# Reading three partial sums back one by one at the end of a decoder layer: wider additions, and a gate product moved ahead of the last slot's turn

## The reference, cut to what matters

```
logits  = h @ gate_w.T; top 4 of 16 experts, weights normalised
shared  = (silu(h @ sg_gate.T) * (h @ sg_up.T)) @ shared_down.T      # 704 wide
shared *= sigmoid(h @ shared_gate_vec.T)
sparse  = sum over experts e: cw[:, e] * (silu(h @ g_e.T) * (h @ u_e.T)) @ down_e.T   # 176 wide
x       = x + shared + sparse
```

## Time and profile before

| what | value |
|---|---|
| median of 3 runs | 1036.52 us (1035.57 to 1037.06) |
| the profiled execution's own time | 1036.78 us |
| its span, first to last instruction | 1035.0 us |
| mean granted TensorE clock | 0.974 of full speed |
| TensorE busy | 964.0 us (93%) |
| VectorE busy | 827.1 us (80%) |
| GpSimd busy | 508.4 us (49%) |
| ScalarE busy | 379.7 us (37%) |

### The profile page before, as it was taken

One profiled execution on the slowest core, in us unless ns is written; L12 is line 12 of the kernel. 1 busy time (PEld: TensorE's weight loads), 2 busy tenths in 40 slices (PEclk: granted clock), 3 DMA queues, 4 the chain that ended last, 5 costly groups with the idle time before them and its releaser, 6 DMA issues.

```text
span 1035.0 us, 17365 instructions
## 1 busy us (share of the span) xinstructions
PE 964.0 (93%) x5569; PEld 852.9 (82%) x5569; DVE 827.1 (80%) x1595; ACT 379.7 (37%) x1063; POOL 508.4 (49%) x384
## 2 busy tenths in 40 slices
PE   4799899999999999999899999978999899999996
PEld 3688788889888887888788888866887799999985
DVE  4989999999889999878899988766576666666637
ACT  2454443533423443233353322341243244444420
POOL 0525344465635245666435667505715166666650
PEclk8899999999999999999999999989999999999999
DMA  9789679997248312203412120323141277777759
GB/s 348 279 326 380 248 270 366 408 344 274 87 148 307 131 62 82 78 27 115 192 61 83 62 83 22 149 95 130 63 184 69 67 122 117 119 121 120 121 78 304
DMA packets 67383, 171.84 MB, mean 166 GB/s; under 512 B 6752, under 2 KB 40288, under 8 KB 66144
## 3 DMA queue, kind: packets, MB, share of 16 engines
q1 hardware_dynamic: 52848, 151.69, 40.1%
q0 software_dynamic: 14448, 19.05, 11.2%
HBM read 84.72 MB, written 85.99 MB: 165 GB/s over the span
## 4 chain that ended last, share of the span: by engine, by line
PE 64%; DVE 25%; issue 5%; DMA 3%; ACT 1%; another core or an unknown queue 1%; SPq 0%; DVEq 0%; POOLq 0%; ACTq 0%
PE bank L469 8%; PE bank L471 8%; PE bank L470 8%; DVE rot L1335 5%; PE bank L549 5%; PE bank L679 4%; DVE rot L1332 4%; PE bank L702 4%; PE bank L818 3%; PE bank L820 3%; PE bank L779 3%; PE bank L572 2%; PE bank L574 2%; PE bank L573 2%; DMA raw<-in_wqkv 2%
## 5 line engine op out<-in xcount | busy, mean ns | idle before, releaser
L1145 POOL TENSOR_TENSOR rot<-turn 64x512 f32<-64x512 f32 x64 | 92.2, 1440 | 258.1 <-DVE turn L1319 232.9
L1319 DVE SCALAR_TENSOR_TENSOR turn<-bank,bqk,trig 128x1024 f32<-128x1024 f32 x128 | 160.7, 1276 | 13.2 <-PE bank L471 11.2
L1213 POOL DMA_INDIRECT sums<-ysb,token_at x79 | 123.1, 1558 | 76.1 <-DVE ysb L1686 37.1
L469 PE MATMUL bank<-xt_hi,w_hi 128*128 128x512 f32 x256 | 106.6, 417 | 16.7 <-DVE turn L1319 11.4
L1178 POOL TENSOR_TENSOR kv<-c_t,v_t 128x512 f32<-128x512 f32 x64 | 69.3, 1099 | 98.3 <-ACT v_t L945 46.0
L679 PE MATMUL bank<-wo,z_t 128*128 128x256 f32 x512 | 116.0, 379 | 0.8 <-ACT z_t L1016 0.8
L679 PEld LDWEIGHTS bank<-wo,z_t 128*128 128x128 f32 x512 | 94.9, 190 | 12.8 <-ACT z_t L1016 1.0
L977 ACT ACTIVATE prob<-prob,negmax 128x128 f32<-128x128 f32 x256 | 98.9, 389 | 6.9 <-DVE negmax L1304 6.8
L471 PE MATMUL bank<-xt_hi,w_lo 128*128 128x512 f32 x256 | 100.7, 393 | 0.0
L470 PE MATMUL bank<-xt_lo,w_hi 128*128 128x512 f32 x256 | 100.5, 392 | 0.0
L987 ACT COPY v<-bank 128x512 f32<-128x512 f32 x64 | 37.6, 587 | 164.6 <-PE bank L471 164.6
(11 more groups left out here) (183 smaller groups left out, 2424.0 us busy)
## 6 DMA issues: line engine op xcount, KB each, us to landing
xs<-zeros SPq DMA_DIRECT2D x12, 3710.0 KB, 17.1
w_hi<-w_dram SPq DMA_DIRECT2D x24, 768.0 KB, 4.7
w_lo<-w_dram SPq DMA_DIRECT2D x24, 768.0 KB, 7.0
xe_all<-xs SPq DMA_DIRECT2D x79, 132.5 KB
sums<-zeros SPq DMA_DIRECT2D x3, 2176.0 KB, 12.5
raw<-in_wqkv SPq DMA_DIRECT2D x16, 384.0 KB, 4.4
w_dram<-w_hi SPq DMA_DIRECT2D x8, 768.0 KB, 5.9
w_dram<-w_lo SPq DMA_DIRECT2D x8, 768.0 KB, 7.3
```

Source lines behind the costliest of these rows:

```text
L469: nc.tensor.matmul(o, lh, rh, start=(i == 0), stop=False)
L1213: nc.gpsimd.indirect_dma_start(sums_dram[s % YBUFS], bass.IndirectOffsetOnAxis(ap=token_at[:, s:s + 1], axis=0), ysb[s % YBUFS][:], None, ...
L1319: last = nc.vector.scalar_tensor_tensor(turn_all[m][:, 2 * i:2 * i + 2, :], qk_bank[2 * m + i][:].unsqueeze(1).to_broadcast([128, 2, GT]), ...
```

## The change

- The reads of the sums follow the landing of each array. The arrays' last slots are 76 (array 1), 77 (array 2) and 78 (array 0). SyncE now waits for array 1, issues four loads of it (four batches, 512 KB each), then the same for array 2 and for array 0. There are 12 loads in place of 24.
- VectorE adds four batches at a time, 12 additions of 128x1024 in place of 24 of 128x512: array 1 behind chunks 1 and 2, array 2 behind chunks 3 and 4 (two additions each), array 0 (four additions) behind chunk 5. A store of x now waits for the third array's addition to its quarter.
- `ysb` has four buffers (YBUFS) while the arrays stay three (SUMS); `slot_out(s)` waits for the landing of slot s - 4.
- The first gate product of the last quarter moves from s = 80 to s = 79, behind `slot_down(77)` and ahead of `slot_turn(78)`; its up product follows `slot_turn(78)`. For that the last quarter's chunks use the other bank of each pair (`shared_bank`), and two waits are set one slot earlier.

```diff
-YBUFS = 3
+YBUFS = 4
+SUMS = 3
+LAST_SUMS = [(SLOTS + i) % SUMS for i in range(SUMS)]
...
+def shared_bank(k, i):
+    return (i + (SLOTS if k == GROUPS - 1 else 0)) % 2
...
-            for i in range(YBUFS):
-                sp.wait_ge(y_stored[i], 16 * ((SLOTS - i + YBUFS - 1) // YBUFS))
-
-            for j in range(BATCH // 2):
-                for i in range(YBUFS):
-                    rows = sums_dram[i][j * 256:(j + 1) * 256, :]
-                    sp.dma_start(ys[j][:, i], rows.rearrange("(b p) d -> p b d", b=2)).then_inc(ys_loaded[j], 16)
-            for j in range(BATCH // 2):
-                sp.wait_ge(comb_done, YBUFS * (j + 1))
-                if 2 * j >= BATCH - GB:
-                    sp.wait_ge(acc_added, 2 * j + 2)
-                sp.dma_start(out[:, 2 * j:2 * j + 2, :], x[:, 2 * j:2 * j + 2, :]).then_inc(stored, 16)
+            for i in LAST_SUMS:
+                sp.wait_ge(y_stored[i], 16 * len(range(i, SLOTS, SUMS)))
+                for j in range(GROUPS):
+                    rows = sums_dram[i][j * GT:(j + 1) * GT, :]
+                    sp.dma_start(ys[j][:, i], rows.rearrange("(b p) d -> p b d", b=GB)).then_inc(ys_loaded[i][j], 16)
+            for j in range(GROUPS):
+                sp.wait_ge(comb_done, GROUPS * (SUMS - 1) + j + 1)
+                for half in range(2):
+                    b = GB * j + 2 * half
+                    if j == GROUPS - 1:
+                        sp.wait_ge(acc_added, b + 2)
+                    sp.dma_start(out[:, b:b + 2, :], x[:, b:b + 2, :]).then_inc(stored, 16)
...
-            def shared_up(k, i):
+            def shared_up(k, i, gates=True, ups=True):
                 n, q = k * SCH + i, SHARED_AT[k]
+                at = shared_bank(k, i)
+                if not gates:
+                    pe.wait_ge(eht_taken, SLOTS - 1)
+                    shared_block(SCH - 1 + i, banks[4 + at], q).then_inc(upb_ready, 1)
+                    return
...
-                if s == SLOTS + 1:
-                    unit(GROUPS - 1, 0)
                 if s >= 2:
                     slot_down(s - 2, experts[(s - 2) % 4])
+                if s == SLOTS:
+                    shared_up(GROUPS - 1, 0, ups=False)
                 if 1 <= s <= SLOTS:
                     slot_turn(s - 1)
+                if s == SLOTS:
+                    shared_up(GROUPS - 1, 0, gates=False)
...
-                if s >= YBUFS:
-                    pool.wait_ge(y_stored[s % YBUFS], 16 * (s // YBUFS))
+                if s >= SUMS:
+                    pool.wait_ge(y_stored[s % SUMS], 16 * (s // SUMS))
...
-                    dve.wait_ge(y_stored[s % YBUFS], 16 * (s // YBUFS))
+                    dve.wait_ge(y_stored[(s - YBUFS) % SUMS], 16 * ((s - YBUFS) // SUMS + 1))
...
-            def combine(j):
-                xj = x[:, 2 * j:2 * j + 2, :]
-                dve.wait_ge(ys_loaded[j], 16 * YBUFS)
-                for i in range(YBUFS):
-                    if i:
-                        dve.wait_ge(comb_done, YBUFS * j + i)
-                    nc.vector.tensor_tensor(xj, xj, ys[j][:, i], ALU.add).then_inc(comb_done, 1)
+            def combine(nth, j):
+                xj = x[:, GB * j:GB * (j + 1), :]
+                dve.wait_ge(ys_loaded[LAST_SUMS[nth]][j], 16)
+                if nth:
+                    dve.wait_ge(comb_done, GROUPS * nth)
+                nc.vector.tensor_tensor(xj, xj, ys[j][:, LAST_SUMS[nth]], ALU.add).then_inc(comb_done, 1)
...
                 shared_mult(GROUPS - 1, i)
-                if i >= 2:
-                    combine(2 * i - 4)
-                    combine(2 * i - 3)
-            dve.wait_ge(comb_done, YBUFS * BATCH // 2)
+                if 1 <= i <= 4:
+                    for j in range(2):
+                        combine((i - 1) // 2, 2 * ((i - 1) % 2) + j)
+            for j in range(GROUPS):
+                combine(SUMS - 1, j)
+            dve.wait_ge(comb_done, SUMS * GROUPS)
             shared_add(GROUPS - 1)
```

More of the change, by code:

```diff
@@ L63, in decoder @@
     rows_dram = nc.dram_tensor("xs", (ROWS, XW), F32, kind="Internal").ap()
-    sums_dram = [nc.dram_tensor(f"sums{i}", (TOKENS + 128, D), F32, kind="Internal").ap() for i in range(YBUFS)]
+    sums_dram = [nc.dram_tensor(f"sums{i}", (TOKENS + 128, D), F32, kind="Internal").ap() for i in range(SUMS)]
     w_dram = nc.dram_tensor("w_dram", (PAIRS, 2, 128, CH, PW), F32, kind="Internal").ap()
@@ L212, in decoder @@
         gctx = ExitStack()
-        ys = [sb(f"ys{j}", [128, YBUFS, 2, D], c=gctx) for j in range(BATCH // 2)]
+        ys = [sb(f"ys{j}", [128, SUMS, GB, D], c=gctx) for j in range(GROUPS)]
         gctx.close()
@@ L329, in decoder @@
         xe_loaded = [sem(f"xe_loaded{i}") for i in range(4)]
-        y_stored = [sem(f"y_stored{i}") for i in range(YBUFS)]
+        y_stored = [sem(f"y_stored{i}") for i in range(SUMS)]
         diag_ready, spread, spread_taken, matched, id_ready = [sem(n) for n in ("diag_ready", "spread", "spread_taken", "matched", "id_ready")]
-        ys_loaded = [sem(f"ys_loaded{j}") for j in range(BATCH // 2)]
+        ys_loaded = [[sem(f"ys_loaded{i}_{j}") for j in range(GROUPS)] for i in range(SUMS)]
         sums_zero = sem("sums_zero")
@@ L404, in _ @@
                         fill(p + 4)
-                    if g == 2 and p < YBUFS:
+                    if g == 2 and p < SUMS:
                         rows = sums_dram[p].rearrange("(n p) d -> p n d", p=128)
@@ L757, in shared_up @@
                         pe.wait_ge(hm_done, n - 1)
[L758 to L761, removed]
+                if k == GROUPS - 1 and i < 2:
+                    pe.wait_ge(eh_done, SLOTS - 1 + i)
+                shared_block(i if i < SCH - 1 else 2 * (SCH - 1), banks[2 + at], q).then_inc(gate_ready, 1)
+                if k == GROUPS - 1 and i == 1:
                     pe.wait_ge(eht_taken, SLOTS)
-                if i < SCH - 1:
+                if i < SCH - 1 and ups:
                     if n > 1:
                         pe.wait_ge(hm_done, n - 1)
-                    shared_block(SCH - 1 + i, banks[4 + i % 2], q).then_inc(upb_ready, 1)
+                    shared_block(SCH - 1 + i, banks[4 + at], q).then_inc(upb_ready, 1)
             def shared_down(k, i):
@@ L1045, in shared_silu @@
                 if i < SCH - 1:
-                    nc.scalar.activation(sg[n % 2][:], banks[2 + i % 2][:], ACT.Silu).then_inc(sg_done, 1)
+                    nc.scalar.activation(sg[n % 2][:], banks[2 + shared_bank(k, i)][:], ACT.Silu).then_inc(sg_done, 1)
                 else:
-                    nc.scalar.activation(sg[n % 2][128 - SLAST:128, :], banks[2 + i % 2][0:SLAST, :],
+                    nc.scalar.activation(sg[n % 2][128 - SLAST:128, :], banks[2 + shared_bank(k, i)][0:SLAST, :],
                                          ACT.Silu).then_inc(sg_done, 1)
@@ L1205, in _ @@
             scatter(last, 0, GB * TOPK)
-            pool.wait_ge(sums_zero, 16 * YBUFS)
+            pool.wait_ge(sums_zero, 16 * SUMS)
             for s in range(SLOTS):
@@ L1210, in _ @@
                 pool.wait_ge(ey_taken, s + 1)
-                if s >= YBUFS:
-                    pool.wait_ge(y_stored[s % YBUFS], 16 * (s // YBUFS))
+                if s >= SUMS:
+                    pool.wait_ge(y_stored[s % SUMS], 16 * (s // SUMS))
                 nc.gpsimd.indirect_dma_start(
-                    sums_dram[s % YBUFS], bass.IndirectOffsetOnAxis(ap=token_at[:, s:s + 1], axis=0), ysb[s % YBUFS][:], None,
-                    compute_op=ALU.add).then_inc(y_stored[s % YBUFS], 16)
+                    sums_dram[s % SUMS], bass.IndirectOffsetOnAxis(ap=token_at[:, s:s + 1], axis=0), ysb[s % YBUFS][:], None,
+                    compute_op=ALU.add).then_inc(y_stored[s % SUMS], 16)
         @block.vector
@@ L1509, in shared_mult @@
                     dve.wait_ge(upb_ready, k * (SCH - 1) + i + 1)
-                    nc.vector.tensor_tensor(hs[n % 2][:], banks[4 + i % 2][:], sg[n % 2][:], ALU.mult).then_inc(hm_done, 1)
+                    nc.vector.tensor_tensor(hs[n % 2][:], banks[4 + shared_bank(k, i)][:], sg[n % 2][:], ALU.mult).then_inc(hm_done, 1)
                 else:
                     h = slice(128 - SLAST, 128)
-                    nc.vector.tensor_tensor(hs[n % 2][h, :], banks[2 + i % 2][h, :], sg[n % 2][h, :], ALU.mult).then_inc(hm_done, 1)
+                    nc.vector.tensor_tensor(hs[n % 2][h, :], banks[2 + shared_bank(k, i)][h, :], sg[n % 2][h, :], ALU.mult).then_inc(hm_done, 1)
             def shared_add(k):
```

## The result

The changed kernel took 1030.14 us (median of 5 runs, 1027.72 to 1031.44) against 1036.52 us (median of 5, 1035.16 to 1037.06). The ratio of the runs compared is 0.995, 95% interval 0.9936 to 0.9964: 5.2 us faster, between 3.7 and 6.6; the two medians themselves lie 6.4 us apart. The prediction was 1032.3 us, a gain of 4.2 us, with a range of 1031.4 to 1034.4. The direction was right and the forecast gain lies inside the interval, but the time itself lies 1.3 us under the range. What follows has to say which part of the difference the change made and which part it didn't.

The account below looks back on a forecast made before the run. VectorE's additions after the last slot's landing were taken to bound the end: `shared_mult(3, 5)` earlier, -4.66 us, wider additions behind it, +0.45, gave -4.2 on 1036.78, 1032.6; the median 0.26 lower, 1032.3 us, range 1031.4 to 1034.4.

Parts of the forecast that it names:

- The prediction's other figure: VectorE's four last wide additions by the Trainium skill's formula, 1224 ns each: 4.90 us rather than 4.65.
- Part 1: Array loads at the end: first issued at 1000.6 rather than 1006.29, all landed by 1022.3.
- Slower: Rival: the load queue delays slot 78's addition, so array 0's loads and VectorE's last additions wait; 1039.7 us, chance 0.03.
- Part 4: TensorE's moved gate product: two more seams with transposes cost 0.1 us, between 0 and 0.2; no gain.
- Part 5: Four `ysb` buffers in the slot stage: worth 0, as `slot_out` never waited for a landing.
- The loads bind: Rival: loads never pass 277 GB/s, the last lands 0.5 us after VectorE wants it; 1032.8 us, chance 0.15.
- Doesn't do what it says: Rival: landings bunch up, first loads leave no earlier, at 1006.3; 2.9 us still gained, 1033.6 us, chance 0.05.
- Head of line: Rival: array 1's additions, waiting for late loads, hold up VectorE's products; up to 1 us, 1033.3 us, chance 0.08 (shared).

Follow-up runs that it names:

- all_landed: The changed kernel with SyncE waiting for all three arrays before the first load: ratio to the kernel before 0.9984, tail 36.71 us.
- before_again: The kernel before with no edit, profiled a second time: 1033.74 us (12 runs), ratio 0.9999, tail 39.11 us.
- pool_adds: The changed kernel with the third array's first two additions on GpSimd: ratio to the kernel before 0.9954, tail 35.04 us.

## Why the prediction was right and wrong

**The mechanism, right.** VectorE was the end before, and the early start of the loads freed it together with the new order of additions: without the early start (`all_landed`) about half of the gain is left. `shared_mult(3, 5)` is released by the silu (forecast) and starts 24.90 us behind slot 77's down product in place of 29.62: -4.72 us, against -4.66. The four additions take 4.63 us against 4.65. The shared term and the tail of the last store stayed: 1023.98 to 1028.1 is 4.12 us, before 1030.82 to 1035.0, 4.18 us. The four also settle the pitch: they start 1.14 us apart and take 1.22 us each. The prediction's other figure, 4.90 us for the four, would have made the sum 0.25 us larger; its "the same to 0.02 us" holds for the duration of one addition only.

**Part 1, the loads.** Right in sum, with the third array later than forecast. The first load went out at 997.89, 4.20 us behind slot 77's product (forecast 1000.6 on the clock of before, 4.36 behind it). The third array's came late, since slot 78's addition took 8.2 us from its start on GpSimd to its landing beside the full load queue, where it had taken 3.84 alone. The view of the DMA issues between 999.5 and 1001 us (KB each, median us to landing):

```profile
ys<-sums SPq DMA_DIRECT2D x2, 512.0 KB, 9.8
sums<-ysb,token_at POOLq DMA_INDIRECT x1, 8.2
```

The mechanism of the rival *Slower* is therefore real: 4.3 us more. It didn't decide, because the queue was still working off the first two arrays, whose last load landed at 1014.89. The third array's first load was issued at 1008.11, when the addition had landed, and itself landed in 8.3 us, at 1016.4; VectorE needed it at 1019.31. The last one, issued at 1012.25 with 8.6 us to landing, was in at 1020.8, 1.9 us before the fourth addition began at 1022.7. The forecast margin was 3 us. In the expectation of `all_landed` the same queue was put at +2.6 to +3.0 us and measured +2.3. The Trainium skill's rule of turns between queues (DMA: Bandwidth & Descriptors, "Queues, rings and completion order"), which the prediction cited, held as far as that the addition did not wait for the whole backlog: it landed at 1008.09, ahead of five of the eight loads issued by then. But its packets began only 5.1 us after GpSimd's start in place of 2.1.

**Part 4**, 0.1 us for the seams: +0.06 us in `slot_down(78)`, 0.06 in the tails with and without the move. **Part 5**, the fourth buffer: 0. Both right.

**What failed: the base of the sum.** The step was "-4.2 us on the profiled execution's 1036.78 ... The median is 0.26 us lower", with "runs scatter by some 0.3 around their median". It put at nothing whatever differs between executions ahead of the tail. In the two traces that was worth 2.55 us, more than half as much as the tail's 4.35. It has three parts. The stretch from the shared product at about 799 us to slot 0 was 3.5 us shorter in the changed kernel (15.9 us for 19.5), and the slots 0.35 us. Against that the changed kernel lost 1.4 us before, nearly all of it between 115 and 140 us: there the granted clock falls to the lower of its two levels for a few us in both, but at another moment (0.91 over 100 to 120 us and 1.00 over 120 to 140 before, the other way round after), and of two instructions of GpSimd that both programs have, the first came 0.13 us earlier than before and the second, 23 us on, 1.26 us later.

Three runs gave a median, and I took its neighbourhood for the scatter. More runs show the kernel before at 1034.3, 1034.6 and 1039.2 us on three chips, with 6 to 7 us from the lowest to the highest run on the first two. From 1034.4 the same sum gives 1030.2, and the changed kernel measured 1030.14 and, on chip 2, 1030.04. A range for a time had to hold what separates chips and executions, and mine held neither.

**And a term a little small.** The sum was made against one execution whose tail was 38.76 us. Four executions give 38.49, 38.76, 39.11 and 39.80, a mean of 39.04, while the changed kernel gave 34.41, 34.41 and 34.40. The gain is 4.6 us on average, a ratio of 0.9955 on 1034.4, inside the intervals of the changed kernel's ratios (0.995 and 0.9949). The term of -4.2 us was 0.4 us small. The spread before comes from the loads: in the third execution the first additions waited 3.42 and 0.53 us for `ys`, in the profile of the prediction 2.85 us and no more. VectorE was full from there on, so each of these waits lengthened the end: they add up to 2.6, 2.85, 3.3 and 3.95 us in the four executions (fourth, first, second, third), and the tail less the waits is 35.8 to 35.9 us in each. The changed kernel has slack at that place: its first additions waited 1.63, 0.28, 0.27 and 0.19 us and it lost nothing.

**The rivals.** *The loads bind* did not happen, but with less to spare than I said (1.9 us for 3). *Doesn't do what it says*: the loads left early; with the start taken away, `all_landed` shows what I put at 2.9 us gained as 1.8 to 3.1. *Head of line*: all four additions of the first array waited for loads, 2.4 us in all. Chunk 2's product came 0.5 us late by it (4.97 us behind chunk 1's in place of 4.46), and still in time for TensorE, which never waited for an `hs`.

What stays open: what ScalarE and VectorE wait for in the stall on chip 0, and whether it belongs to the chip or to the time; and whether the first two profiled executions came from one chip, which their record doesn't say. A first ratio of 0.995 where the tails give 0.9955 needs no other cause.

## What to carry to other kernels

Loads that stand behind the last landing of everything can be split by what each of them needs, and the work on them ordered so that no instruction depends on the one just before it. Here the early start gave one half of the gain. The order and the width of the additions gave the other, the width 0.2 to 0.6 us of it; how the rest divides was not tried. A tail counted between two marks repeated to 0.01 us in the changed kernel and within 1.3 us in the kernel before, where medians on different chips stood 5 us apart: give a forecast as a difference, and let the range of an absolute time hold what separates chips and executions.

## What the runs showed of the hardware that I had not expected

- An indirect addition beside a queue of 512 KB loads landed 8.2 us after its start on GpSimd (`after`), 3.84 us without them (`before`).
- The same loads took 8.3 to 10.3 us to land once the queue was full, and SyncE's issue of one took up to 2.03 us in place of 0.38 to 0.63.
- One stretch, the same in all these programs, took 15.8 to 16.7 us on two chips and 21.3 to 21.4 us on a third, in each execution there. In the first execution of the kernel before, where it took 19.5 us, a silu started 5.3 us later than in `before_again`, with its product done at the same time.
- Additions of two SBUF operands on VectorE and GpSimd side by side (`pool_adds`): 8.2 us for VectorE's four and 6.6 us for GpSimd's two, where VectorE alone did four in 4.63 us; one of VectorE's took 3.40 us in place of 1.22.
